# First stage of batches 2 and 3 in pieces beside the tiles, tokens turned by PE: a fused convolution and scan kernel

## The reference

```python
theta_x = conv1x1(x, w_theta, b_theta).reshape(b, c, n).transpose(0, 2, 1)
phi_x = conv1x1(x, w_phi, b_phi).reshape(b, c, n)
g_x = conv1x1(x, w_g, b_g).reshape(b, c, n).transpose(0, 2, 1)
out = jnp.matmul(jnp.matmul(theta_x, phi_x) / n, g_x)   # then w_rec, batch norm, + x
```

## Time and profile before

| | |
|---|---|
| median of 3 runs | 5504.55 us (5501.18 to 5506.01) |
| the profiled execution's own time | 5506.06 us |
| its span | 5504.3 us |
| DVE busy | 5058.5 us (92%) |
| POOL busy | 5044.1 us (92%) |
| PE busy | 4768.9 us (87%) |
| ACT busy | 3552.7 us (65%) |
| end of the prologue (POOL's next instruction) | 270.7 us |
| first scan to the start of the last program | 316.6 to some 5459 us |
| mean granted TensorE clock | 0.938 of full |

### The profile page before, as it was taken

The page is one execution under the profiler, slowest core; times in us unless marked ns, Lnnn a source line. Parts: engine busy times, 40 slices in busy tenths (PEclk is TensorE's granted clock), DMA queues, the critical chain, the costliest instruction groups (busy, mean ns, idle before and its releaser), DMA issues. The chain is left out here.

```text
span 5504.3 us, 70129 instructions
## 1 busy us (share of the span) xinstructions
PE 4768.9 (87%) x25566; PEld 3445.4 (63%) x25566; DVE 5058.5 (92%) x3463; ACT 3552.7 (65%) x5626; POOL 5044.1 (92%) x2469
## 2 busy tenths in 40 slices
PE   8878888888888888888888898889999999999987
PEld 7846566666666656566656666666666666666665
DVE  4469999999999999999999999999999999999995
ACT  0057676766676667676776676767676767676762
POOL 0079999999999999999999999999999999999994
PEclk9989998999999999999999999999999999999998
DMA  4222323232323232323142424242424242424242
GB/s 157 103 91 85 103 80 107 76 108 74 111 72 111 72 115 68 118 65 118 65 128 81 131 82 131 82 137 90 133 91 132 94 131 93 132 93 135 89 135 100
DMA packets 223005, 567.00 MB, mean 103 GB/s; under 512 B 28258, under 2 KB 94690, under 8 KB 221508
## 3 DMA queue, kind: packets, MB, share of 16 engines
q1 hardware_dynamic: 210996, 532.78, 29.7%
q10 hardware_dynamic: 11664, 29.74, 1.4%
HBM read 501.08 MB, written 61.36 MB: 102 GB/s over the span
## 5 line engine op out<-in xcount | busy, mean ns | idle before, releaser
L1066 POOL TENSOR_TENSOR dbx<-dtx,b_all 128x896 f32<-128x896 f32 x1792 | 3719.8, 2116 | 74.9 <-DMA b_all<-bc_scratch 71.6
L1012 DVE TENSOR_TENSOR_SCAN mamba_ps<-mamba_ps,dbx 128x896 f32<-128x896 f32 x1232 | 2483.6, 2016 | 50.1 <-POOL dbx L1066 41.3
L802 PE MATMUL mamba_ps<-ident,hc 128*112 128x128 f32 x14336 | 1887.6, 285 | 558.8 <-POOL hc L1073 545.8
L802 PEld LDWEIGHTS mamba_ps<-ident,hc 128*112 128x112 f32 x14336 | 1675.9, 139 | 850.8 <-POOL hc L1073 606.5
L857 ACT ACTIVATE mamba_ps<-dt,a_next 128x448 f32<-128x448 f32 x1792 | 1069.0, 629 | 633.4 <-DVE hc L1019 517.2
L857 ACT ACTIVATE mamba_ps<-dt,w 128x448 f32<-128x448 f32 x1792 | 1067.4, 629 | 635.3 <-DVE hc L1019 510.0
L1019 DVE TENSOR_TENSOR hc<-mamba_ps,c_all 128x896 f32<-128x896 f32 x1232 | 1342.3, 1090 | 144.7 <-DVE mamba_ps L1012 3.9
L1073 POOL TENSOR_TENSOR hc<-hc,c_all 128x896 f32<-128x896 f32 x560 | 1183.5, 2114 | 0.0
L1012 DVE TENSOR_TENSOR_SCAN hc<-mamba_ps,dbx 128x896 f32<-128x896 f32 x560 | 1123.7, 2015 | 42.8 <-ACT mamba_ps L857 39.9
L697 PE MATMUL mamba_ps<-u,w 128*128 128x448 f32 x1792 | 805.8, 592 | 18.6 <-DMA u<-u_scratch 15.3
L708 PE MATMUL mamba_ps<-x,taps 128*128 128x448 f32 (+3 forms) x1792 | 683.6, 529 | 1.0 <-ACT sz L880 0.5
(11 more groups left out here) (111 smaller groups left out, 2978.7 us busy)
## 6 DMA issues: line engine op xcount, KB each, us to landing
b_all<-bc_scratch SPq DMA_DIRECT2D x448, 448.0 KB, 5.3
c_all<-bc_scratch SPq DMA_DIRECT2D x448, 448.0 KB, 6.4
u<-u_scratch SPq DMA_DIRECT2D x56, 448.0 KB, 3.3
y_scratch<-ytok SPq DMA_DIRECT2D x56, 448.0 KB, 3.3
src<-y_scratch SPq DMA_DIRECT2D x47, 448.0 KB, 5.3
u_scratch<-ub ACTq DMA_DIRECT2D x28, 448.0 KB, 4.7
src<-in_x SPq DMA_DIRECT2D x27, 448.0 KB, 6.7
xb<-in_x ACTq DMA_DIRECT2D x3, 3136.0 KB, 11.8
```

What stands on the lines that cost most here:

```text
L802: ins = nc.tensor.matmul(y_ps[j % 2][:, c * 128:(c + 1) * 128], hc[n % HC_RING][:, e * T + c * TCH:e * T + (c + 1) * TCH], ident[:, :], st ...
L1012: nc.vector.tensor_tensor_scan(dst, h, dbx[n % BX_RING][:, :], 0.0, ALU.mult, ALU.add).then_inc(scan_done, 1)
L1066: nc.gpsimd.tensor_tensor(view(dbx[n % BX_RING], 0, [[T, 2], [1, T]]), view(dtx, j * T, [[0, 2], [1, T]]), view(b_all, 2 * g * T, [[T, 2], ...
```

## The change: what it does

The prologue keeps only batches 0 and 1 (`HERE`). Its blocks have 128 positions, so a pass has 12 whole pairs and one block of 64. Weight groups move forward. u stays in image order: `second_half` is seven pieces of 448 positions, K stationary and x moving, ACT adds the bias, SP stores to `u_image`. For batches 2 and 3, `PLAN` puts pieces into tiles 0 to 18, up to two a tile (place a and place b): seven `gram` pieces, one `small` step (K and the biases) and seven `image` pieces a batch. Their items a0, a1, a2, b0, b1, b2 are in `SCHEDULE`. ACT loads each piece's x, or the weights, into the unused `src` when the piece before has been read (`load_job`), evacuates the items and stores the image. Tokens of every tile of the first Mamba block are loaded by SP from the image order (`load_tokens`, token-major), turned by PE two tiles ahead (`turn_tokens`, items t0 and t1, eight transposes), copied by ACT into u and stored to `u_scratch` (`save_u`) for the second block. The first tiles' tokens are turned ahead of tile 0 (`PRELUDE`).

```diff
+    "out1": (17, 20), "dt0": (19, 21), "dt1": (21, 23), "dt2": (21, 23), "dt3": (23, 23), "t0": (24, 24), "y1": (25, None), "a0": (25, 26),
+    "f0": (26, 26), "a1": (26, 28), "f1": (26, 29), "a2": (29, 29), "t1": (29, 29), "b0": (30, 30), "b1": (30, 30), "y2": (31, None),
+    "b2": (31, 31),
 }
 FRONT = ("x0", "x1", "c0", "c1", "x2", "x3", "c2", "c3", "xp", "dt0", "dt1", "dt2", "dt3")
 BACK = ("y3", "out0", "out1")
+TURN = ("t0", "t1")
...
+PLAN = {
+    0: (("gram", 2, 0), ("gram", 2, 1),),
+    1: (("gram", 2, 2),),
...
+    5: (("gram", 2, 6),),
+    6: (("small", 2, 0),),
+    7: (("image", 2, 0), ("gram", 3, 0),),
+    8: (("image", 2, 1), ("gram", 3, 1),),
...
+    13: (("gram", 3, 5), ("gram", 3, 6),),
...
+JOBS = {(t, place): job for t, jobs in PLAN.items() for place, job in zip("ab", jobs)}
+ORDER = sorted(JOBS)
+ITEMS = {"gram": 3, "small": 3, "image": 2}
...
+                def take_piece(q):
+                    b, i = pieces[q]
+                    upto(act, u_stored[q % RING], 16 * (q // RING))
+                    for oc in range(2):
+                        act.wait_ge(ut_ready, 2 * q + oc + 1)
+                        nc.scalar.activation(uo[q % RING][:, oc * T:(oc + 1) * T], bank(6 + oc)[:, 0:T], ACT.Identity,
+                                             bias=kn[b][:, 2 * CH + 2 + oc:2 * CH + 3 + oc]).then_inc(ut_taken, 1)
...
+                    pe.wait_ge(k_dve, 3 * b + 3)
+                    for i in range(TPB):
+                        q = TPB * HERE.index(b) + i
+                        for oc in range(2):
+                            upto(pe, ut_taken, 2 * q + oc - 1)
+                            for k in range(2):
+                                last = nc.tensor.matmul(bank(6 + oc)[:, 0:T], kn[b][:, k * CH + oc * 128:k * CH + (oc + 1) * 128],
+                                                        xb[b][:, k * NPOS + i * T:k * NPOS + (i + 1) * T], start=(k == 0), stop=(k == 1))
+                            last.then_inc(ut_ready, 1)
+                        if then is not None and i == 0:
...
+        PRELUDE = [(0, n) for n in TURN + FRONT[:8]] + [(1, n) for n in TURN] + [(0, n) for n in FRONT[8:]]
...
+                def load_tokens(t):
+                    if t > 0:
+                        sp.wait_ge(work_ready, Item(t - 1, "t1").ready())
+                    if t // TPB not in HERE and t % TPB == 0:
+                        sp.wait_ge(u_out, 16 * sum(JOBS[k][0] == "image" and JOBS[k][1] <= t // TPB for k in ORDER))
+                    sp.dma_start(utok.rearrange("p (c f) -> p c f", c=4), u_tok[t // TPB, t % TPB]).then_inc(tok_ready, 16)
+
+                def save_u(t):
+                    for name in TURN:
+                        it = Item(t, name)
+                        sp.wait_ge(work_free[it.slot], it.freed())
+                    sp.dma_start(u_dram[t], u[t % 2][:, :]).then_inc(u_saved[t % 2], 16)
+
                 for t in range(2):
-                    load_u(t)
+                    load_tokens(t)
+                sp.dma_start(s1w, s1_dram).then_inc(s1_in, 16)
+                sp.dma_start(now[:, :], k_dram[1]).then_inc(here_in, 16)
+                save_u(0)
...
+                    if t + 1 < TILES:
+                        save_u(t + 1)
+                    if t + 2 < TILES:
+                        load_tokens(t + 2)
...
+                def turn_tokens(t, k):
+
+                    if k == 0:
+                        pe.wait_ge(tok_ready, 16 * (t + 1))
+                    b = take(Item(t, f"t{k}"))
+                    for c in range(4):
+                        ins = nc.tensor.matmul(b[:, c * TCH:(c + 1) * TCH], utok[:, c * FEAT + k * 128:c * FEAT + (k + 1) * 128],
+                                               ident[0:TCH, 0:TCH], start=(c == 0), stop=(c == 3), is_transpose=True, skip_group_check=True)
+                    ins.then_inc(work_ready, 1)
+
+                def add_gram(t, place, k, i):
+                    it = Item(t, f"{place}{k}")
+                    if k < 2:
+                        b = take(it)
+                        nc.tensor.matmul(b[0:TCH, 0:512], ones[:, :], view(src, 2 * T + J_BIAS, [[0, 2], [1, 256]], 1),
+                                         start=True, stop=False, skip_group_check=True)
+                        for h in range(2):
+                            c = 2 * k + h
+                            for kk in range(2):
+                                ins = nc.tensor.matmul(b[0:TCH, h * 256:(h + 1) * 256], xs[:, kk * T + c * TCH:kk * T + (c + 1) * TCH],
+                                                       s1w[:, kk * 256:(kk + 1) * 256], start=False, stop=(kk == 1), skip_group_check=True)
+                    else:
+                        for h in range(2):
+                            half = Item(t, f"{place}{h}")
+                            pe.wait_ge(work_free[half.slot], half.freed())
+                        b = take(it)
+                        if i > 0:
+                            nc.tensor.matmul(b[:, 0:CMID], ident[:, :], acc[:, :], start=True, stop=False)
+                        for c in range(4):
+                            s = pg[c // 2][:, c % 2 * 256:(c % 2 + 1) * 256]
+                            ins = nc.tensor.matmul(b[:, 0:CMID], s[:, 128:256], s[:, 0:128], start=(i == 0 and c == 0), stop=(c == 3))
+                    ins.then_inc(work_ready, 1)
+
...
+                def make_image(t, place, oc, b):
+                    if oc == 0:
+                        if b in (0, 1):
+                            pe.wait_ge(here_in, 16)
+                        else:
+                            made = next(k for k in ORDER if JOBS[k][0] == "small" and JOBS[k][1] == b)
+                            it = Item(made[0], f"{made[1]}2")
+                            pe.wait_ge(work_free[it.slot], it.freed())
+                    bank = take(Item(t, f"{place}{oc}"))
+                    for k in range(2):
+                        ins = nc.tensor.matmul(bank[:, 0:T], now[:, k * CH + oc * 128:k * CH + (oc + 1) * 128], xs[:, k * T:(k + 1) * T],
+                                               start=(k == 0), stop=(k == 1))
+                    ins.then_inc(work_ready, 1)
+
...
+                def load_job(q):
+                    if q < len(ORDER):
+                        kind, b, i = JOBS[ORDER[q]]
+                        if kind == "small":
+                            act.dma_start(xs[:, 0:K_R], kw_dram).then_inc(job_in, 16)
+                        else:
+                            act.dma_start(xs.rearrange("p (k n) -> p k n", k=2),
+                                          x_in[b].rearrange("(k p) n -> p k n", p=128)[:, :, i * T:(i + 1) * T]).then_inc(job_in, 16)
...
+                def take_job(t, name):
+                    kind, b, i = JOBS[t, name[0]]
+                    q, k, it = ORDER.index((t, name[0])), int(name[1]), Item(t, name)
+                    if kind == "gram":
+                        if k < 2:
+                            nc.scalar.copy(pg[k], take(it)[0:TCH, :]).then_inc(work_free[it.slot], 1)
+                        else:
+                            nc.scalar.copy(acc[:, :], take(it)[:, 0:CMID]).then_inc(work_free[it.slot], 1)
+                        if k == 1:
+                            load_job(q + 1)
+                    elif kind == "small":
+                        if k == 0:
...
+                    else:
+                        if k == 0:
+                            upto(act, u_out, 16 * images_before(q))
+                        nc.scalar.activation(res[:, k * T:(k + 1) * T], take(it)[:, 0:T], ACT.Identity,
+                                             bias=now[:, 2 * CH + 2 + k:2 * CH + 3 + k]).then_inc(work_free[it.slot], 1)
+                        if k == 1:
+                            load_job(q + 1)
+                            for oc in range(2):
+                                it = Item(t, f"{name[0]}{oc}")
+                                act.wait_ge(work_free[it.slot], it.freed())
+                            act.dma_start(u_img[b].rearrange("(k p) n -> p k n", p=128)[:, :, i * T:(i + 1) * T],
+                                          res[:, :].rearrange("p (k n) -> p k n", k=2)).then_inc(u_out, 16)
+
```

408 lines of the change are left out of this document (234 added, 174 removed), and 2 rows, old and new, of the table SCHEDULE.

## The result

| | before | after |
|---|---|---|
| median, range of the runs | 5504.68 us (5501.18 to 5506.01) | 5413.97 us (5407.95 to 5416.98) |
| the profiled execution's own time, span | 5506.06, 5504.3 us | 5407.95, 5406.2 us |
| first scan | 316.6 us | 189.85 us |
| tiles 0 to 27 | 2563.0 us | 2590.65 us |
| mean granted TensorE clock | 0.938 | 0.949 |

The ratio is 0.9836, 95% interval 0.9822 to 0.9849: 91 us less, where 95 were forecast. The profiled execution took 6 us less than the median of its four runs. Its span is 98.1 us shorter: the first scan comes 126.8 us earlier, tiles 0 to 27 last 27.6 longer, tiles 28 to 54 last 0.9 longer, and 0.2 us more lie behind them.

A forecast was written before the change was run, and what follows sets the result against it. The prediction saw a serial PE stretch first, then tiles with DVE and POOL at 96% and more. 5506.1 - 123.0 + 4.9 + 22.3 = 5410.3 us for the profiled execution, 5409 against the median; range 5392 to 5445.

The forecast's parts named there:

- part one: Prologue: only fourteen pieces follow the two passes, so it ends at 147.7 instead of 270.7, shorter by 123.0 us.
- part two: Way from the prologue to the first scan: turning and copying the first tokens adds 4.9 us, bounds 3 to 8.
- part three: Tiles: place b costs 31.2 us, 8.9 us are given back, so 22.3 us are added.
- Both together: no change: Prologue passes of batches 0 and 1: fewer pairs offset the added weight groups, so passes end at 95.
- Place a and the tokens cost nothing: Tiles: tokens and a whole Gram piece, 8.3 us, fit where PE idles 6.68 us until POOL's product, at no cost.
- copies a1 until 2317.3 and issues: Tile 21, slot 28: ACT issues place b's load after copying a1; landing at 2321.9, Gram 3.6 us late, image 1.3.
- With work in place b PE doesn't idle there: Tile's end: half of ACT's 1.08 us wait for x0, about 0.6 us, comes back in 11 tiles.
- rival B: The clock falls before place b while PE waits for the load: 73 us more, so 5482; chance 0.10.
- a slot or 3.1 us later: 4.4: Tile 14: place b's load is issued only in slot 29, so the tile loses 4.4 us.
- Given back: Tiles: 8.9 us return, 6.6 in 11 tiles with place b and 2.3 in 15 other tiles with turned tokens.
- A: Rival: nothing of place b shows, part three is only the gift, 5378 us; chance 0.07.
- C: Rival: PE becomes the bound, every added matmul lengthens its tile, 180 us added, 5567 us; chance 0.03.

The follow-up runs named there:

- the replanned kernel: The changed kernel with the same thirty pieces in another order, Gram in place a wherever possible: 5383.39 us median, ratio 0.9776; with a later load of batch 1's x 5383.33 us.
- e4: The changed kernel with place a's last PE step repeating its matmuls three times in tiles with an image: 5400.02 us.
- e12: The changed kernel with ACT loading batch 1's x only once the first matrix's weights have landed: 5409.31 us median, ratio 0.9830.
- e13: The changed kernel itself timed once more, unaltered, on the same chip as its version with the wait: 5410.64 us median, ratio 0.9830.
- e8: The changed kernel with no load for place b, which works on the x that place a loaded (output not the reference's): 5388.20 us.

## Why the prediction was right, point by point

The mechanism held: a serial stretch of PE became 14 pieces, place a and the tokens nearly vanished in PE's gaps, and what is lost in the tiles is lost in place b, ahead of y2. That the total is as close as 5409 against 5414 (5410.3 against 5407.95 for the profiled execution) is in part luck. For the profiled execution part one came out 7.5 us better than forecast, outside its bounds, part two 1.2 better, part three 5.3 worse and what lies behind tile 27 1.1 worse; these add up to 2.3.

*Part one, the prologue.* 130.5 us gained, not 123.0 (end at 140.23, not 147.7), outside its bounds of 119 to 127. The passes end at 92.4 instead of 95. All of the 2.6 come from batch 0's pass, which ends at 58.28 for 60.95 before; batch 1's lasts 34.1 us in both (0.5 less was forecast). "A piece is four matmuls of 448 columns, 3.17 us for 8 records" took the length of a row, whose end overlaps the next one's start: in the same place before the change the next matmuls start at 287.54, 3.01 us behind 284.53. Back to back a piece is these 3.01 us, and the 44.4 + 2.6 became 44.1 with the small matrices. The last copy, store and landing took 3.8 us, not 5.7. Of "Both together: no change" the block size was tested (6.3 for 6.5). PE's wait for the weights, 7.96 us here and 5.28 before, ends at nearly the same time in both (35.53 and 36.20) and so is no gain and no loss.

*Part two, the way to the first scan.* +3.7 us (49.6 against 45.9) for +4.9. x0 starts 6.4 us behind the prologue's end for 3.3 before, +3.1 (forecast 2.9). x_proj, at 32.5 behind it for 26.6 before, is 5.9 later (forecast 4.9). So the mechanism cost 1 us more than forecast; then 2.2 came back that no term held, most of it in dt_proj, whose eight records took 3.40 us for 5.30 before.

*Part three, the tiles.* +27.6 us for +22.3. The parts are 37.0 more in slots 29 and 30, 1.2 more in tile 0, 9.8 less in slots 0 and 0.8 less elsewhere. "Place a and the tokens cost nothing" holds for Gram and image pieces; but tile 0 takes 1.2 us more and a small step 0.2 to 1.9 in slot 29. Place b was put at 31.2 and took 36.4 (the 37.0 without 0.6 of tile 6's small step), by steps of which three failed:

- "copies a1 until 2317.3 and issues": ACT issues the load 1.79 us before slot 28, not at 0.05 behind its start. The transfer is sent while the engine still has exponentials and the copy itself to do (issue at 910.25, the copy of a1, which stands ahead of it in the program, at 911.37). The landing takes 3.5 to 5.6 us, for the 4.5 taken. So x is there 1.7 to 3.9 us behind the start of slot 28, not 4.65, and PE is free by then too. At the upper level of the clock a Gram costs 2.0 us instead of 3.6 and an image nothing instead of 1.3, as Gram behind Gram, the run with more work on PE and the replanned kernel measure.
- "With work in place b PE doesn't idle there", and against rival B "place a fills just that gap": a Gram in place a fills it, an image does not. In the seven tiles with an image in place a PE idled 4.2 to 5.5 us, and the granted clock fell to 0.50 before b in each. This put 2.4 us on each Gram and 1.9 on each image. Rival B thus came true in these tiles, at a third of its price: only part of place b ran at 1.2 GHz, x had come sooner, and what B took as lost, the gain in slot 0, came back (below).
- "a slot or 3.1 us later: 4.4" for tile 14: 9.9 us. ACT issues the load 5.95 us behind slot 28, not 3.15. The small step's last matmuls came at 1573.43, 4.3 us into slot 28 (PE does its sums in between, and the granted clock was 0.50 from 1565 to 1571.5), and the store of the matrices is issued first; then eight records took 5.81 us instead of 3.27.

"Given back" was right in its larger part, and this is what made up for place b. Slot 0 lasts 3.16 us where PE makes x0 at the full clock and up to 1.6 us more where it doesn't. In the eleven tiles behind a place b (1 and 8 to 17) the time over 3.16 adds up to 7.04 us before the change, and to 0.03 us in each of the four profiles with this plan and order (after, e4, e12, e13): 7.0 given back, for 6.6. With tokens alone it is 7.6 and with place a alone 5.2, so it is place b that gives it. The other 2.3 can't be told: in the sixteen remaining tiles from 1 to 27 the same sum is 8.5 before, 5.7 here, and 5.6 to 8.0 in the other three. Much of what tiles without pieces vary by, 90.7 to some 92 us, is this slot.

The Trainium skill ("DMA: Bandwidth & Descriptors", "Issuing engines are not separate DMA queues") has transfers of all issuers interleave on the same engines. For the load in place b the measured 4.8 us stands against the slow bound drawn from it. The profiles of the start agree with it: weights on SP's queue came late in six of eight with ACT's 3.2 MB in flight beside them, and in none of the three in which that load was issued behind them.

*Rivals.* A (nothing of place b shows, 5378) is what a different plan comes near to (5383). C (PE the bound, 5567) is out: PE is busy 121 us more in tiles 0 to 27 and they last 28 longer; with place a alone it is busy 60 us more than with tokens alone, and tiles 0 to 27 last the same within 0.4 us.

One argument under B can be settled, whether the identity transposes hold the clock up. In the kernel before the granted clock was 0.50 from 1120.3 to 1123.6 us, PE did nothing there but the sums' transposes, and from 1123.7 on it was 1.00:

```profile
1120.65 3.39 PE L802 MATMUL mamba_ps<-ident,hc 128*112 128x128 f32 x16 [2.54 <-POOL hc L1073]
1123.88 1.04 PE L794 MATMUL mamba_ps<-skip,x 128*112 128x128 f32 x8
```

*Signs named ahead.* Single-job tiles came at 90.7 to 92.0, tile 0 at 96.5 for 94.5, tiles 7, 8, 9 at 94.8 to 95.5 for 94.5, 10, 11, 15, 16 at 92.2 to 93.3 for 92.2; tiles 12 and 13 at 92.7 and 93.0, not 94.5; the first scan at 189.85, not 198.5; DVE's gate waits for PE's y2, as said. Of the signs against it one showed, in tile 0 alone: the gap behind the table loads of slot 25, 1.03 us.

The best kernels here are the replanned ones, 5383.4 and 5383.3 us, 0.5 to 0.6% under the changed kernel and 2.2% under the one before.

## What to carry to other kernels

Work that is put into another engine's gaps is free where its input is there and dear where it waits: ask of each place what ran on PE in the microseconds before it, since the same Gram cost 2 us behind work, 4.4 behind idle time and up to 10 when the lower clock covered all of it. Look behind the place too: work there can keep the clock up for what follows, which gave back 7 us here. Pair pieces so that the long one runs while the next one's load is in flight, and put nothing behind a step that delays that load. Before moving a step ahead of a wait, ask which buffer it then holds and who frees it; here holding the gate's bank cost more than the late gate. And when a forecast comes true, compare it term by term: here two misses of 7.5 and 5.3 us stood against each other.

## What the runs showed of the hardware that was not expected

- ACT issues a DMA ahead of work that its engine still has to do: at 910.25, when an exponential had just started at 910.24, and the copy ahead of the load in the program ran at 911.37.
- PE's clock can fall just behind a wait, under running matmuls. After 3.07 us of idle time, tile 7 of e4 ran all of place b at 1.2 GHz (clock 0.63 over 16.4 us); after 1.72 us tile 8 ran it at 2.4 GHz; after 1.59 us tile 9 fell all the same. In e8 1.70 and 1.69 us of idle time were followed by 0.54 and 0.81 on average. Idle time in one wait alone doesn't tell.
- Identity transposes by themselves bring PE's clock up: 0.50, then 1.00 from 1123.7 us on, behind 3 us in which PE did nothing else.
- How long a tile without pieces takes, 90.7 to some 92 us, goes in good part by the clock at which PE makes x0 in its slot 0: nothing is lost at 1.00, up to 1.6 us below.
- With the same code up to there, loads of weights landed by 28 or only at 33.4 to 35.7 us. With another queue's 3.2 MB issued at 27.2 to 28.0 instead of 22.0 to 23.0 us it was 28 in three runs of three, and PE didn't wait for that load.
